# A graph-conv block and an inverted bottleneck on sixteen images: the rolled image loop written out as one straight program

## What is computed

```python
# layer 0
y = affine(conv1x1(x, fc1_w, fc1_b), fc1_s, fc1_t)
nodes = windows(y)                                   # 1024 windows of 64 nodes, 96 channels
idx = top_k(-dist(nodes / norm(nodes)), 9)
feat = concat([x_i, x_j - x_i])                      # each node with its 9 neighbours
h = max_k(gelu((feat @ ew.T + eb) * es + et))
x = affine(conv1x1(unwindow(h), fc2_w, fc2_b), fc2_s, fc2_t) + x
# layer 1
h = relu(bn(conv1x1(x, w1)))                         # 576 channels
h = relu(bn(depthwise3x3(h, wd)))
out = x + bn(conv1x1(h, w2))
```

## Time and profile before

| | |
|---|---|
| runs | 4085.14, 4085.38 and 4087.81 us |
| profiled execution | 4088.99 us |
| its span, first to last instruction | 4087.1 us |
| mean granted TensorE clock | 0.987 |
| TensorE busy | 3900.1 us (95%) |
| VectorE busy | 3821.1 us (93%) |
| ScalarE busy | 3698.3 us (90%) |
| GpSimd busy | 931.4 us (23%) |

### The profile page before, as it was taken

One profiled execution on the slowest core, in us unless ns is written; L12 is line 12 of the kernel. 1 busy time (PEld: TensorE's weight loads), 2 busy tenths in 40 slices (PEclk: granted clock), 3 DMA queues, 4 the chain that ended last, 5 costly groups with the idle time before them and its releaser, 6 DMA issues.

```text
span 4087.1 us, 79112 instructions
## 1 busy us (share of the span) xinstructions
PE 3900.1 (95%) x22752; PEld 2050.5 (50%) x22752; DVE 3821.1 (93%) x5162; ACT 3698.3 (90%) x6806; POOL 931.4 (23%) x1060
## 2 busy tenths in 40 slices
PE   6999999999999999999999999999999999999984
PEld 3445555455555555555554555545555455555442
DVE  3699999999999999999999999999999999999996
ACT  4899999899998999999999999989999899999983
POOL 1122222222222222222222222122222122222113
PEclk9999999999999999999999999999999999999996
DMA  2133333333433333342333333333342333333333
GB/s 60 24 65 71 67 76 65 72 62 66 79 62 67 63 77 66 65 84 50 79 69 67 67 74 66 64 72 70 59 85 54 68 69 68 78 64 58 62 66 65
DMA packets 100116, 272.34 MB, mean 67 GB/s; under 512 B 14946, under 2 KB 23394, under 8 KB 93476
## 3 DMA queue, kind: packets, MB, share of 16 engines
q0 software_dynamic: 65536, 184.58, 26.4%
q1 hardware_dynamic: 34116, 82.27, 7.5%
HBM read 77.68 MB, written 25.69 MB: 25 GB/s over the span
## 4 chain that ended last, share of the span: by engine, by line
PE 70%; DVE 10%; ACT 9%; issue 9%; DMA 1%; ACTq 0%; POOL 0%; DVEq 0%; POOLq 0%; SPq 0%
PE pg L651 18%; PE pmisc L579 9%; PE pg L654 9%; PE pvu L638 8%; PE pmisc L565 7%; DVE acc L1043 7%; PE pmisc L522 3%; PE pmisc L515 2%; PE pvu L624 2%; ACT MV L813 2%; PE pmisc L581 2%; PE pmisc L545 2%; DVE hid L1021 2%; PE pmisc L550 2%; ACT tapped L850 1%
## 5 line engine op out<-in xcount | busy, mean ns | idle before, releaser
L1043 DVE SCALAR_TENSOR_TENSOR acc<-hpad,w,acc 128x1024 f32<-128x1024 f32 (+1 forms) x2304 | 2615.8, 1159 | 34.6 <-issue 17.5
L651 PE MATMUL pg<-MV,VU 128*128 128x512 f32 x2048 | 1150.6, 644 | 40.5 <-ACT VU L821 29.7
L830 ACT ACTIVATE g<-pg 128x512 f32<-128x512 f32 x1536 | 913.2, 595 | 131.3 <-PE pg L654 81.2
L1021 DVE TENSOR_REDUCE hid<-g 128x192 f32<-128x1536 f32 x512 | 891.9, 1742 | 0.0
L430 POOL DMA_DIRECT2D acc<-tapped x256 | 240.9, 941 | 2108.5 <-DVE acc L1043 1824.3
L813 ACT ACTIVATE MV<-pvu,cst 64x512 f32<-64x512 f32 x1024 | 696.5, 680 | 11.9 <-PE pvu L624 5.0
L579 PE MATMUL pmisc<-acc,w 128*96 128x256 f32 x2048 | 497.4, 386 | 50.5 <-ACT acc L860 35.4
L654 PE MATMUL pg<-MV,VU 128*64 128x512 f32 x2048 | 527.7, 592 | 0.0
L565 PE MATMUL pmisc<-x,w 96*128 96x512 f32 (+1 forms) x1024 | 515.4, 605 | 8.8 <-ACT hpad L772 8.8
L638 PE MATMUL pvu<-wVU,y 97*64 97x192 f32 x4096 | 447.4, 340 | 22.0 <-ACT MV L813 21.7
L579 PEld LDWEIGHTS pmisc<-acc,w 128*96 128x96 f32 x2048 | 331.5, 165 | 263.8 <-issue 155.9
(11 more groups left out here) (102 smaller groups left out, 4447.8 us busy)
## 6 DMA issues: line engine op xcount, KB each, us to landing
acc<-tapped POOLq DMA_DIRECT2D x256, 512.0 KB, 4.9
xin<-in_x_dram SPq DMA_DIRECT2D x32, 768.0 KB, 5.7
invb<-rows_dram SPq DMA_DIRECT2D x32, 768.0 KB
x<-in_x_dram POOLq DMA_DIRECT2D x128, 192.0 KB, 4.1
res<-x POOLq DMA_DIRECT2D x128, 192.0 KB, 5.1
out_dram<-res SPq DMA_DIRECT2D x128, 192.0 KB, 3.2
hpad<-hpad SPq DMA_DIRECT2D x112, 33.0 KB, 1.8
g<-in_consts_dram SPq DMA_DIRECT2D x1, 640.0 KB
```

What stands on the lines that cost most here:

```text
L651: last = nc.tensor.matmul(ps[:, :], VU[:, r, part, 0:ONE128], cols[part], start=True, stop=True)
L830: nc.scalar.activation(g[:, p % 2, part, :, :], pg[(3 * p + part) % 2][:, :].rearrange("p (n k) -> p n k", k=KN), ACT.Gelu).then_inc(gelu_ ...
L1021: nc.vector.tensor_reduce(hid[:, c % 2, j, :, :], g[:, r], op=ALU.max, axis=AX.X).then_inc(hid_ready, 1)
L1043: nc.vector.scalar_tensor_tensor(out=dst, in0=src, scalar=wk, in1=dst, op0=ALU.mult, op1=ALU.add).then_inc(tap_done, 1)
```

## The change

The sixteen images are issued by a Python loop, so the hardware loop is gone on all five engines, and the image number is a constant everywhere.

```diff
         def image_loop(eng, image, tail):
 
             image(-1, 16, PAIRS)
-            image(0, 0, PAIRS)
-            with eng.Fori(1, B - 2, 2) as b:
+            for b in range(B):
                 image(b, 0, PAIRS)
-                image(b + 1, 0, PAIRS)
-            image(B - 1, 0, PAIRS)
             image(B, 0, tail)
```

## The result

| | before | changed |
|---|---|---|
| median of the runs, us | 4086.12 (4085.14 to 4087.81, 4 runs) | 4032.54 (4031.99 to 4033.62, 4 runs) |
| profiled execution, us | 4088.99 | 4031.99 |
| its span, us | 4087.1 | 4030.2 |
| mean granted clock | 0.987 | 0.991 |

The changed kernel takes 0.9869 of the time (95% interval 0.9852 to 0.9886).

The account below looks back on a forecast made before the run. TensorE and VectorE in turn were taken to set the pace, TensorE's jump stops lying on the path. Profiled 4088.99 less 39.0 for jumps, nothing for register instructions or fetch, gave 4050.0; half the run offset made it 4048 us, range 4040 to 4060.

Parts of the forecast that it names:

- The stops: TensorE idle on issue at the scores' matmul after each of six loop jumps, 22.1 us in all.
- Both ways of pricing them: Jump cost from TensorE's idle plus slow clock, 38.3 us, and from image windows, 39.0 us or 6.5 a jump.
- the price of a branch that it quoted: The Trainium skill's 108 ns per compare-and-branch, by which the loop costs under 1 us and the change does nothing.
- First-time code in sequence: Instruction fetch for the longer straight program: full speed, costed at nothing, at most 1 to 2 us new.
- the slow clock comes anyway: Rival: TensorE's clock stretches come from dense work, so 16.2 us stay; gain 22.8, time 4064 us; chance 5%.
- the one that ends slower: Rival: TensorE's fetch of straight code falls behind at packets; 4126 us at 0.5 us each; chance 3%.
- One sign of being right: VectorE's work per image was to stay unchanged at 237.6 us.
- the image length: Sign: images 2 to 14 all at 243 to 244.5 us between their reduces, odd and even alike.
- Register instructions: Their removal from every wait of fourteen images, costed at nothing; bounds 0 and 1.3 us of gain.
- the two single waits of the earlier trace: VectorE's wait for TensorE's scores in pairs 7 to 11, 0.60 us in loop code and 0.59 in straight code.
- register arithmetic was on the path: Rival: TensorE's sequencer causes a third of VectorE's 6.4 us idle per image; 28 us more, 4020 us; chance 4%.
- half of the 3.6 us as luck at the jumps: The runs' median lay 3.6 us below the profiled execution; half was carried over, turning 4050.0 or 4046.4 into 4048 us.

Follow-up runs that it names:

- the step put back: Changed kernel plus, in every pair, one TensorE semaphore increment nobody waits for, between the wait for vu_evac and the gather's first matmul: 4049.82 us.
- the moved wait: Kernel before, all loops kept, with TensorE's wait for gelu_done moved ahead of those for onehot_ready and vu_evac: 4079.98 us, ratio 0.9987.

## Why the prediction was off

**What held.** The stops are where the prediction put them, on TensorE, behind its branch. Both ways of pricing them gave 38.3 and 39.0 us, and taking away five of six gave 31.9 us (4084.77 to 4052.91), where 32.5 were due. The prediction counted three engines' branches as agreeing with the price of a branch that it quoted; the earlier trace rows has four, at 40 to 63 ns, about half of that price, and VectorE too stood idle on issue for 2.1 to 3.2 us behind each of its six jumps:

```profile
DVE acc L1043 <- issue: 17.5, 12, 3.2
```

TensorE's stop covered that: with only TensorE in its loop VectorE has no jump, and the time falls by 4.2 us at most. The slow clock went with the stops: in 3154 us of straight program there is none. First-time code in sequence brought no stop; the rival "the slow clock comes anyway" and the one that ends slower are both refuted. The order of the work did not change, and the other engines' jumps and register instructions together cost the 3.2 us (by windows 4.1) by which the kernel with only TensorE straight stays behind. One sign of being right failed beside the image length: VectorE's work per image is 236.75 us in the mean, not the 237.6 that was to stay.

**What failed: the step "Register instructions", costed at nothing with a bound of 1.3 us.** It is 1.16 us an image, 15.1 us in images 2 to 14. The step concluded from pairs 7 to 11, 39.43 against 39.44 us, that no register instruction was on the path. Those five pairs can't show it. VectorE is busy for 38.8 of their 39.4 us, and their windows are drawn by VectorE's reduces, so they measure VectorE. The kernel with the step put back, which is 17.3 us slower, shows the same time there as the changed kernel (first row: changed, second: step put back):

```profile
3489.72:3529.15 39.43, 38.40 (x224) 19.58 (x223) 38.77 (x54) 38.60 (x76) 9.62 (x10) 1.00 0.36 73
```

```profile
3504.11:3543.54 39.43, 38.08 (x223) 19.35 (x222) 38.77 (x54) 38.60 (x75) 9.61 (x10) 1.00 0.37 73
```

In this stretch TensorE falls behind by 0.26 us, in its pairs 10 and 12, and it is paid outside the window (by VectorE's pairs of image 14 mostly in 5, 12 and 28), above all where VectorE waits for scores (150.3 us in 163 waits with the step put back, 140.6 in 148 in the changed kernel). In all twelve traces of this case, from 4029 to 4117 us of span, the stretch takes 39.43 or 39.44 us. Where two engines set the pace in turn, a stretch in which one of them is full is blind to the other's losses. The same holds for the two single waits of the earlier trace rows: that wait is 0.59 or 0.60 us in all twelve traces. The reading of "the sequencers do their arithmetic while the engines work" holds nearly for register instructions ahead of the wait that comes last (with the moved wait an image is within 0.3 us of the changed kernel's), and fails for those behind it; the order of instructions before had one behind `vu_evac` in each of 64 pairs of the body, and the prediction never looked at which wait came last.

The rival "register arithmetic was on the path" was the true one, at half of its price: it had a third of VectorE's 6.4 us of idle, and it is 1.16 of them.

**The offset between the profiled execution and the runs.** I took half of the 3.6 us as luck at the jumps. The straight program's profiled execution is 0.55 us below its median, and its runs spread over 1.6 us, those of before over up to 9. The kernels without a jump on TensorE spread over 1.6 to 2.6 us in four runs each, so the jumps are likely what spread the others. The forecast was 2.5 us too low by this alone (2.0 taken off where 0.55 were to be added), and 15.5 in all too high: the forecast for the profiled execution, 4050.0 against 4031.99 us, was 18 us off, and luck hid a part of it.

## What to carry over

Price a hardware loop on its sequencers one by one: the jump of the engine that sets the pace, with the clock behind it, and each register instruction that stands behind a wait that comes last. A count that a later wait needs should be worked out, and that wait be made, ahead of the wait that is late; here one instruction of 51 ns behind it cost 17 us over the 512 pairs of the run. And check a claim of "costs nothing" on a whole period of the kernel, not on a stretch in which another engine is full.

## What the runs showed of the hardware

A taken jump back cost TensorE's sequencer 4.4 to 7.6 us of branch in all kernels, while the branch records of VectorE, ScalarE, GpSimd and SP showed 40 to 90 ns in all of theirs. The short record is not the whole price: in the kernel before, VectorE's next idle time on issue, 2.1 to 3.2 us, ended 5.4 to 6.5 us after its branch began. The length of the body didn't matter: with one image the branch took 5.5 to 6.0 us, with seven 5.6. TensorE idled for 2.9 to 5.0 us of it in the kernel before, and the 1.2 GHz stretches at its jumps lasted 3.4 us or 6.8 us; over all kernels one lasted 10.2 us (the moved wait), and three jumps had none (the first one of two kernels, and one with one image in the body).

Between the release of a wait and TensorE's matmul, a sequencer instruction lengthened the way by two to three times its own duration: the increment of 51 ns by 0.16 us (0.74 against 0.58 us from the start of VU's copy in pair 11), the register instruction of 37 ns by 0.10 us (0.73 against 0.63 us with it moved ahead).
